# Rotary rotation of queries and keys: two half-height VectorE products in place of a TensorE product and one VectorE product

## The reference, cut to what matters

```
def _rotate_half(x):
    x1, x2 = jnp.split(x, 2, axis=-1)
    return jnp.concatenate([-x2, x1], axis=-1)
def _apply_rope(x, cos, sin):
    return x * cos[None, None] + _rotate_half(x) * sin[None, None]
...
q = _apply_rope(q, cos, sin)
k = _apply_rope(k, cos, sin)
attn = softmax(einsum('bhid,bhjd->bhij', q, k) * scale)
```

## Time and profile before

| what | us |
|---|---|
| median of 3 runs | 3167.82 |
| lowest and highest of them | 3150.28 and 3169.93 |
| the profiled execution | 3159.59 |
| its span, first to last instruction | 3157.7 |
| its mean granted TensorE clock | 0.937 |

### The profile page before, as it was taken

How to read it: one execution, slowest core, us unless ns; L and a number is a source line. 1 busy time by engine, 2 the same in 40 slices (tenths; PEclk the granted TensorE clock), 3 DMA queues, 4 the chain that set the end, 5 groups by cost and what they waited for, 6 DMA issues and landing times. The chain is left out here.

```text
span 3157.7 us, 56651 instructions
## 1 busy us (share of the span) xinstructions
PE 2744.4 (87%) x18875; PEld 2089.5 (66%) x18875; DVE 2522.5 (80%) x3552; ACT 2238.8 (71%) x4092; POOL 2166.7 (69%) x1633
## 2 busy tenths in 40 slices
PE   5999999939999977889888888888888887769995
PEld 3555555528999834666666666766666666669995
DVE  5688888743444446999999999999999999967895
ACT  2677777522222249999999999999989999656652
POOL 3357667542333348999999999999999999743322
PEclk7899999859999988999999999999999999889996
DMA  6555656426666662222322222222222222324333
GB/s 141 105 110 114 118 115 117 78 68 194 189 197 190 166 220 81 77 77 72 85 81 83 78 71 85 81 83 81 70 82 81 82 79 72 107 62 124 92 105 111
DMA packets 221306, 333.24 MB, mean 106 GB/s; under 512 B 34902, under 2 KB 130220, under 8 KB 216394
## 3 DMA queue, kind: packets, MB, share of 16 engines
q1 hardware_dynamic: 210722, 310.39, 37.1%
q0 software_dynamic: 9280, 18.38, 1.9%
q10 hardware_dynamic: 1008, 0.72, 0.1%
HBM read 274.11 MB, written 59.27 MB: 106 GB/s over the span
## 5 line engine op out<-in xcount | busy, mean ns | idle before, releaser
L1809 POOL TENSOR_TENSOR resid_x<-s_ux,s_B_rows 128x1024 f32<-128x1024 f32 x256 | 605.4, 2365 | 89.8 <-PE s_y L2539 89.1
L2370 DVE TENSOR_TENSOR_SCAN resid_x<-s_dA,resid_x 128x1024 f32<-128x1024 f32 x256 | 582.0, 2274 | 33.0 <-ACT s_dA L2021 22.9
L2378 DVE TENSOR_TENSOR_SCAN resid_x<-s_late,s_back_in 128x1024 f32<-128x1024 f32 x256 | 583.6, 2280 | 20.9 <-ACT s_late L2031 16.3
L2539 PE MATMUL s_y<-identity,resid_x 128*128 128x128 f32 x4096 | 558.4, 281 | 11.3 <-issue 5.4
L2539 PEld LDWEIGHTS s_y<-identity,resid_x 128*128 128x128 f32 x4096 | 498.3, 146 | 67.3 <-issue 35.6
L1817 POOL TENSOR_TENSOR resid_x<-resid_x,s_C_rows 128x1024 f32<-128x1024 f32 x192 | 454.1, 2365 | 0.2 <-DVE resid_x L2370 0.2
L799 DVE TENSOR_REDUCE a_row_max<-a_maxscores 128x2 f32<-128x512 f32 x512 | 338.5, 683 | 71.9 <-PE a_maxscores L1023 68.7
L2385 DVE TENSOR_TENSOR resid_x<-resid_x,s_C 128x1024 f32<-128x1024 f32 x320 | 382.4, 1195 | 6.5 <-PE s_C L2514 6.5
L2526 PE MATMUL s_back_in<-identity,resid_x 128*128 128x128 f32 x2048 | 291.4, 288 | 101.4 <-ACT resid_x L2042 53.0
L2021 ACT ACTIVATE s_dA<-s_dt,s_A 128x510 f32<-128x510 f32 x512 | 329.9, 675 | 69.7 <-DVE resid_x L2370 68.1
L2031 ACT ACTIVATE s_late<-s_dt,s_A 128x510 f32<-128x510 f32 x512 | 338.1, 710 | 0.0
(11 more groups left out here) (479 smaller groups left out, 5635.6 us busy)
## 6 DMA issues: line engine op xcount, KB each, us to landing
s_B_rows<-forward_rows SPq DMA_DIRECT2D x256, 256.0 KB, 3.4
e_w<-L_ffn_w_by_expert SPq DMA_DIRECT2D x71, 768.0 KB, 4.5
s_C_rows<-forward_rows SPq DMA_DIRECT2D x192, 256.0 KB, 3.4
a_Q<-split_qk SPq DMA_DIRECT2D x96, 192.0 KB
split_qk<-a_parts SPq DMA_DIRECT2D x32, 384.0 KB
e_x<-slot_inputs SPq DMA_DIRECT2D x71, 132.0 KB, 2.1
a_K<-split_qk SPq DMA_DIRECT2D x64, 128.0 KB
s_late<-choice_outputs SPq DMA_DIRECT2D x16, 512.0 KB, 5.0
```

The source lines that it names most:

```text
L1809: tt(R[s, 0], ux[par][:], brow[s % BRING][:].unsqueeze(1).broadcast_to([P, C2, W]), ALU.mult).then_inc(S["in_ready"], 1)
L2370: nc.vector.tensor_tensor_scan(r, a, r, 0.0, ALU.mult, ALU.add).then_inc(S["scanned"], 1)
L2378: nc.vector.tensor_tensor_scan(r[:, ::-1], a[:, ::-1], b[:, ::-1], 0.0, ALU.mult, ALU.add).then_inc(S["scanned"], 1)
L2539: last = mm(YP[:, t, c2 * P:(c2 + 1) * P], R[s, d][:, c2, t * P:(t + 1) * P], core.ident[:], is_transpose=True, start=((s, d) == (0, 1) an ...
```

## The change

The matrix `a_rot`, its load and the product L1135 go, with the semaphore `rot_ps` and PE's three waits for `sin_done`. The table of sines gets the sign and is rolled by 64 rows on the host. DVE now forms `a_qk_sin` in two products of 64 partitions by 512 elements: the first writes partitions 0 to 63 from partitions 64 to 127 of `a_qk` and of the table, the second the reverse. The first stands ahead of the row maximum of head 8, the second behind it. DVE's first half waits for `k_ready` (ACT has written the keys). The line numbers of all code behind line 915 shift by up to 7.

```
-                for t, n in (..., (rot, "rope_rot")):
+                for t, n in ((w_uvg, "L0_attn_w_uv_by_group"), (w_o, "L0_attn_w_o_by_group")):
...
-                        at(act, S["rot_ps"], i)
+                        at(act, S["sin_done"], i)
...
+                def half_turned(to):
+                    of = P // 2 - to
+                    return tt(qsin[to:to + P // 2, :], qk[of:of + P // 2].rearrange("p a t -> p (a t)"), sin[of:of + P // 2, :], ALU.mult)
...
+                    if live(i, 0):
+                        dve.wait_ge(S["k_ready"], i + 1)
+                        at(dve, S["roped_ready"], i)
+                        half_turned(0)
                     row_max(i, 8)
                     if live(i, 0):
-                        dve.wait_ge(S["rot_ps"], i + 1)
-                        at(dve, S["roped_ready"], i)
-                        tt(qsin[:], PP[:], sin[:], ALU.mult).then_inc(S["sin_done"], 1)
+                        half_turned(P // 2).then_inc(S["sin_done"], 1)
...
-                        at(pe, S["sin_done"], min(i, B))
...
-                        at(pe, S["sin_done"], i)
...
-                        mm(PP[:], rot[:], qk[:].rearrange("p a t -> p (a t)"), start=True, stop=True).then_inc(S["rot_ps"], 1)
...
-                        at(pe, S["sin_done"], min(i + 1, B))
...
+    out["rope_sin"][:D // 2] *= -1
+    out["rope_sin"] = np.roll(out["rope_sin"], D // 2, axis=0)
```

More of the change, by code:

```diff
@@ L139, in load_and_modulate @@
     nc, B, aps = core.nc, core.B, core.aps
-    kept = {n: core.sbuf("a_" + n, [P, D], on=first) for n in ("w_dk", "w_dv", "w_uk", "w_uv", "w_uv_by_group", "w_o", "rot", "w_k", "w_v")}
+    kept = {n: core.sbuf("a_" + n, [P, D], on=first) for n in ("w_dk", "w_dv", "w_uk", "w_uv", "w_uv_by_group", "w_o", "w_k", "w_v")}
     for n, shape, dt in (("bias_kv", [P, 2], F32), ("bias_cols", [P, 4], F32), ("bias_out", [P, TC * D], F32), ("bias_out_row", [1, D], F32),
@@ L148, in load_and_modulate @@
     s_x = kept["x_loaded"] = [core.sem(f"x_loaded{k}") for k in range(len(LOTS))]
-    w_dk, w_dv, w_uk, w_uv, w_uvg, w_o, rot, w_k, w_v, bias_kv, bias, bo, bo_row, bo_in, ones1, cos, sin = (kept[n] for n in (
-        "w_dk", "w_dv", "w_uk", "w_uv", "w_uv_by_group", "w_o", "rot", "w_k", "w_v", "bias_kv", "bias_cols", "bias_out", "bias_out_row", "b_o_row",
+    w_dk, w_dv, w_uk, w_uv, w_uvg, w_o, w_k, w_v, bias_kv, bias, bo, bo_row, bo_in, ones1, cos, sin = (kept[n] for n in (
+        "w_dk", "w_dv", "w_uk", "w_uv", "w_uv_by_group", "w_o", "w_k", "w_v", "bias_kv", "bias_cols", "bias_out", "bias_out_row", "b_o_row",
         "ones_row", "cos", "sin"))
@@ L207, in _ @@
             def _(act):
-                for t, n in ((w_uvg, "L0_attn_w_uv_by_group"), (w_o, "L0_attn_w_o_by_group"), (rot, "rope_rot")):
+                for t, n in ((w_uvg, "L0_attn_w_uv_by_group"), (w_o, "L0_attn_w_o_by_group")):
                     act.dma_start(t[:], aps[n]).then_inc(S["w_loaded"], 16)
@@ L237, in _ @@
                 columns(0)
-                pe.wait_ge(S["w_loaded"], 16 * 16)
+                pe.wait_ge(S["w_loaded"], 16 * 15)
                 for k, t in enumerate((w_dk, w_dv)):
@@ L435, in attention @@
         sb = lambda name, shape, dt=F32: core.sbuf("a_" + name, shape, dt, on=on)
-        w_o, rot, w_k, w_v, bias_kv, bo, cos, sin = (kept[n] for n in ("w_o", "rot", "w_k", "w_v", "bias_kv", "bias_out", "cos", "sin"))
+        w_o, w_k, w_v, bias_kv, bo, cos, sin = (kept[n] for n in ("w_o", "w_k", "w_v", "bias_kv", "bias_out", "cos", "sin"))
         K9, V, mod_rows, sgn = (kept[n] for n in ("K9", "V", "rows", "sgn"))
@@ L478, in attention @@
             "modrows_ready", "modrows_stored", "lot_var", "lot_ln", "lot_std", "rest_done", "gate_loaded0", "gate_loaded1", "xn_ready", "hT_ps", "hT_ready",
-            "kv_ps", "k_ready", "v_ready", "rot_ps", "cos_done", "sin_done", "roped_ready", "part0",
+            "kv_ps", "k_ready", "v_ready", "cos_done", "sin_done", "roped_ready", "part0",
             "left1", "part1", "part2", "stored", "max_ps", "max_done", "maxT_ps", "max_hi", "max_lo",
@@ L3242, in shape_constants @@
     out["rope_sin"] = np.tile(np.sin(emb).astype(np.float32).T, (H, 1))
-    rot = np.zeros((D, D), np.float32)
-    for m in range(D):
-        half = DH // 2
-        rot[m + half if m % DH < half else m - half, m] = -1 if m % DH < half else 1
-    out["rope_rot"] = rot
     order = dim_major()
@@ L3250, in shape_constants @@
         out[n] = out[n][order]
-    out["rope_rot"] = out["rope_rot"][order][:, order]
+    out["rope_sin"][:D // 2] *= -1
+    out["rope_sin"] = np.roll(out["rope_sin"], D // 2, axis=0)
     out["selector"] = np.tile(np.eye(BC, dtype=np.float32), (PARTS, 1))
```

## The result

The changed kernel takes 3314.22 us (median of 8 runs, 3292.95 to 3359.9) against 3164.89 us before (8 runs beside them, 3144.32 to 3169.93). The ratio is 1.0482, with a 95% interval of 1.045 to 1.0514: nearly 5% slower. I had forecast 3172 us and a range from 3148 to 3196.

The account below looks back on a forecast made before the run. DVE was taken to bound the place in odd heavy turns, PE's product in even and light ones. Terms: 6.6 + 4.4 - 1.0 - 1.9 = +8.1 us on a base of 3163.7, giving 3172 us, range 3148 to 3196.

Parts of the forecast that it names:

- The clock: Rival: a PE with less to do stays one turn longer at 1.2 GHz, costing 5.6 us: 3177 us; chance 0.09.
- lost in waits: Odd heavy turns: PE's later raw scores wait longer for DVE, so PE's gain of 0.96 us brings nothing.
- Odd heavy turns, +0.60: 11 turns: DVE sets the place, the half ahead of head 8 delays it by 0.60 us each, bounds +0.30 and +0.70.
- my bound of 0.70: High bound, in us, for the cost of each half on a busy DVE, taken as 0.60.
- The 0.68 us for the length of a half: On DVE: each half lasts 0.68 us, as the whole product did, since columns set the price and partitions don't.
- Even heavy turns, +0.40: 11 turns: DVE's half and its port wait outweigh PE's earlier scores, +0.40 us each, bounds -0.2 and +1.2.
- +0.7: Even heavy turns: first half waits for POOL's L625, so head 8 starts at about 376.0 instead of 375.29 us.
- The wait of L832 that I took as given back: Even heavy turns: part of L832's wait of about 0.7 us goes, since L832 comes later in POOL's addition or behind it.
- Light turns, -0.2: 5 turns: DVE's room of 0.76 us takes the first half, head 8 starts 0.16 us earlier; bounds 0 and -0.96.
- Turn 4, -1.9: Turn 4, partly at half clock with DVE little busy: PE's 1.86 us are gained; bounds 0 and -1.9.
- PE decides everywhere: Rival: PE's product is on the path in every turn, 27.8 us back: 3136 us; chance 0.12 including cheap halves.
- The port decides: Rival: both halves of every heavy turn wait for POOL products, 2.24 us per heavy turn: 3210 us; chance 0.09.

Follow-up runs that it names:

- after_again: The changed kernel run once more with no edit, its second profiled execution: 3306.93 us, ratio 1.047 against the kernel before.
- product_back: The changed kernel with one unused TensorE product of the old size put back at the old place: 3205.54 us, ratio 1.0135.
- fillers: The changed kernel with two unused 128x256 TensorE products ahead of the raw scores of heads 10 and 11, from turn 4: 3184.56 us, ratio 1.0086.
- one_product: The changed kernel with one unshifted full-height DVE product in place of the two halves, no TensorE product: 3178.88 us, ratio 1.0081.
- first execution: The first profiled execution of the changed kernel, with no further edit, the slowest of its runs: 3359.9 us.
- warm_end: The kernel before with two unused 128x256 PE products in its late 1.32 us wait for a_K: 3149.31 us, ratio 0.9967.

## Why the prediction was wrong

**The step that failed.** I read "the granted clock is 1.00" in turns 7, 19 and 20 and took it for a condition of the stage, under which a pause of PE costs its own length. It was a result of how little PE paused. The sum takes every term but turn 4's at full clock. The clock stood among the rivals, but as one turn more at 1.2 GHz at the start, +5.6 us; it measured an end of attention 144 to 191 us later, with 321 to 453 us more at 1.2 GHz. Less the 17 us that the halves cost at full clock, that is (144.3 - 16.6) / 321 = 0.40 us per low microsecond, and 0.39 in the other execution.

**Both halves of the change were needed for it.** PE's product alone taken away: +0.8%. The halves added, PE's work restored: +1.4%. Both: +4.8%. The sum of the two effects alone is less than half of that. My own text had the two pieces side by side: in odd turns the gain of 0.96 us is "lost in waits", and the row maxima come 0.60 us later. The 0.97 us which PE no longer works, plus the 0.84 us by which the turn grows (17.43 to 18.27), is 1.8 us more idle per turn (0.39 to 2.20), and I wrote it down as free.

**Odd heavy turns, +0.60: measured +0.97** (18.27 against 17.30, in after_again, product_back and fillers alike). The mechanism was right: DVE sets this place, PE's gain goes into waits, and PE's wait for row maxima grew, at heads 9 and 10 and not only at 11. The size missed three late starts of 0.10 to 0.12 us each from the jump between partitions, above my bound of 0.70. The 0.68 us for the length of a half was right (0.69).

**Even heavy turns, +0.40: measured +0.97** with PE's work kept in. The first part came as forecast: in turn 24 of the run with the fillers DVE's first half waits for POOL's L625 (which ends at 456.95 us, the half 0.57 us later), and head 8's row maximum comes 8.23 us into the turn instead of 7.48, +0.75 us where I had +0.7. PE's product was on the path to that point, as one_product shows (6.63 us), but not for the turn: without it, the turn got no shorter. The terms that failed are those behind it, of which I had taken 0.3 us back. POOL does wait for DVE as well, as the rows of the same turn show, DVE first, then POOL:

```profile
455.96 1.56 DVE L919 TENSOR_TENSOR a_qk_sin<-a_qk,a_sin 64x512 f32<-64x512 f32 x1
457.45 0.68 DVE L799 TENSOR_REDUCE a_row_max<-a_maxscores 128x2 f32<-128x512 f32 x1
458.16 0.69 DVE L919 TENSOR_TENSOR a_qk_sin<-a_qk,a_sin 64x512 f32<-64x512 f32 x1
```
```profile
456.88 1.23 POOL L514 TENSOR_TENSOR a_choice_rows<-a_choice_rows,a_mod_rows_b 128x256 f32<-128x256 f32 x1
458.21 1.22 POOL L520 TENSOR_TENSOR a_choice_rows<-a_choice_rows,a_mod_rows_b 128x256 f32<-128x256 f32 x1
```

The first half lasts 1.56 instead of 0.69 us, and L514 and L520 1.23 and 1.22 us instead of some 0.75. The wait of L832 that I took as given back was not: it still took 1.01 us at 459.69 us of the same turn. So DVE and POOL do hold each other up in even turns, by 0.87 us at the first half. How much of the 0.97 us this makes, no run isolates.

**Light turns, -0.2: measured +0.1** (16.52 against 16.40 at full clock in turn 7). PE's busy time fell to 15.36 of 16.52 us, and the freed time is idle. **Turn 4, -1.9:** 25.28 and 20.03 us against 22.03, with the clock at 0.50 throughout in the first execution: the gain is covered by how the clock happened to run.

**The rivals.** "PE decides everywhere" fell in one_product. "The port decides" named 3210 us, the nearest number, by a mechanism that the runs do not bear out at that size: it asked for 2.24 us per heavy turn with a wait at both halves; with the clock held the turns grew by 0.97; the second half waited in no heavy turn, and in odd ones the first did not either. What I had counted as slower by over 1% had a chance of 0.09.

**What in the rows of before could have warned.** The waits between PE and DVE, 40.4 and 30.3 us in turn, together with PE's small rest of 0.4 to 0.6 us a turn, say that PE is kept busy by DVE being just fast enough. And the trace of before has a fall of its own in late turns, at 597.2 us behind a single wait of 1.32 us for a transfer, which made turn 33 take 25.29 us. Its timeline of PE there, where the values (L1050) go from 0.64 to 1.08 us:

```profile
593.86 0.64 PE L1050 MATMUL a_out<-a_probs,a_V 128*32 128x256 f32 x8
594.42 0.71 PE L1167 MATMUL a_proj<-a_w_o,a_oT 128*128 128x128 f32 x4
596.46 0.39 PE L1023 MATMUL a_maxscores<-a_K,a_Q 72*128 72x256 bf16 x2 [1.32 <-DMA a_K<-split_qk]
...
597.58 1.08 PE L1050 MATMUL a_out<-a_probs,a_V 128*32 128x256 f32 x8
```

I priced turn 4's low clock and did not ask what had brought it about.

The Trainium skill, "TensorE: Matmul & The Clock Gate", section "A second HAM failure mode: psum-queue depth-cycling", tells of a kernel whose PE rests briefly but often between groups of matmuls and whose clock goes up and down for it. This case agrees: rests of 0.6 to 0.9 us, a few in a turn, with matmuls between them, are followed by 3 to 58 us at the lower clock at a time.

## What to carry to other kernels

Taking work off a TensorE that waits for another engine was no saving here, and it can cost the clock: before such a change, add up PE's idle time per turn as it will be afterwards, removed work and added waits together, and treat a clock of 1.00 as something that can be lost. To tell this from a plain longer queue, put unused matmuls into the new pauses; if the time comes back, it was the clock. On DVE, a tile of half height cost what the full one did (0.69 us for 512 columns), and each jump between the halves of the partitions from one instruction to the next delayed a start by 0.11 us, so choose the order with the fewest jumps.

## What the hardware showed beyond that

- The clock's answer is not the same from one time to the next: behind the same three pauses it fell in turn 11 and held in turn 13, and low time in two executions of one kernel was 543.9 and 412.0 us.
- Filling the pauses worked, work ahead of them much less: 256 unused columns ahead of the pauses did nothing (477.0 us low), inside them they brought it to 218.9, twice as many to 90.8. 512 columns ahead of them left 145.7.
- A PE without pauses doesn't bring the clock back at once: turn 16 of the second execution ran 29.36 us at 1.2 GHz with PE busy throughout. Why a stretch lasts 23.9 us in one case and 51.2 in another, the runs don't tell.
- What was left open: why a transfer comes later in some executions (the wait of 1.53 us in warm_end ahead of turn 16 is not there in the trace of before), behind which the clock can fall.
